# Three orders in the gated delta rule's groups: half a projection, gate 3 and the second sweep's copy moved

## What is computed

```python
qkvz = x @ W_qkvz                                     # per group: q, k, 2 x v, 2 x z
qkv = jax.nn.silu(_causal_conv1d(qkv, conv_weight))   # 4 taps
q = _l2norm(q) * Dk ** (-0.5); k = _l2norm(k)
decay_mask = jnp.exp(jnp.clip(g[..., :, None] - g[..., None, :], -30.0, 30.0))
attn = -(jnp.einsum('bhcid,bhcjd->bhcij', k_beta, k) * decay_mask)   # lower triangle
attn, _ = jax.lax.scan(_correct_row, attn, jnp.arange(1, chunk_size))  # (I + A)^-1
value_corrected = jnp.einsum('bhcij,bhcjd->bhcid', attn, v_beta)
def chunk_step(state, c): ...                         # a recurrence over the chunks
core = _rmsnorm(core * jax.nn.silu(z), norm_weight)
out = core.reshape(Bx, Sx, VAL_DIM) @ W_out
```

## Time and profile before

| | us |
|---|---|
| Timed runs, median of 3 | 1745.14 (1734.08 to 1746.89) |
| The profiled execution | 1761.52 |
| Its span, first to last instruction | 1759.8 |
| PE busy in the span | 1443.5 |
| VectorE busy | 1135.3 |
| ScalarE busy | 852.7 |
| GpSimd busy | 781.1 |

### The profile page before, as it was taken

How to read it: one execution, slowest core, us unless ns; L and a number is a source line. 1 busy time by engine, 2 the same in 40 slices (tenths; PEclk the granted TensorE clock), 3 DMA queues, 4 the chain that set the end, 5 groups by cost and what they waited for, 6 DMA issues and landing times. The chain is left out here.

```text
span 1759.8 us, 38626 instructions
## 1 busy us (share of the span) xinstructions
PE 1443.5 (82%) x14345; PEld 1032.2 (59%) x14345; DVE 1135.3 (65%) x2336; ACT 852.7 (48%) x2401; POOL 781.1 (44%) x1116
## 2 busy tenths in 40 slices
PE   5988982378624798999999999999999999986665
PEld 2543341245412466677677677777767767775465
DVE  5885138622456576787786787787778778743623
ACT  2335851132113555656655656766665665643122
POOL 6000000465201464665555555666467556453343
PEclk9999995588867898999999999999999999978688
DMA  8100005165613534645555555554464554432783
GB/s 284 54 2 2 1 4 147 31 195 166 216 53 71 129 93 124 161 117 150 142 150 117 140 151 120 151 160 113 140 173 119 152 149 127 107 92 76 202 266 126
DMA packets 249435, 218.74 MB, mean 124 GB/s; under 512 B 88770, under 2 KB 224962, under 8 KB 247200
## 3 DMA queue, kind: packets, MB, share of 16 engines
q1 hardware_dynamic: 234992, 192.41, 39.8%
q0 software_dynamic: 5712, 15.60, 2.7%
q10 hardware_dynamic: 8544, 8.26, 1.5%
HBM read 133.85 MB, written 82.25 MB: 123 GB/s over the span
## 5 line engine op out<-in xcount | busy, mean ns | idle before, releaser
L1674 PE MATMUL d_big<-all_xn_t,all_w 128*128 128x512 f32 x512 | 264.2, 649 | 27.8 <-DVE d_conv L1892 21.4
L1892 DVE SCALAR_TENSOR_TENSOR d_conv<-d_big,all_cw,d_conv 128x1023 f32<-128x1023 f32 (+2 forms) x192 | 245.4, 1278 | 48.0 <-ACT d_conv L2056 45.6
L2242 POOL TENSOR_TENSOR d_y<-d_y,all_xn 128x256 f32<-128x256 f32 x128 | 96.0, 750 | 183.6 <-DVE d_y L2033 153.2
L1674 PEld LDWEIGHTS d_big<-all_xn_t,all_w 128*128 128x128 f32 x512 | 98.3, 207 | 119.6 <-issue 97.0
L2156 ACT COPY d_ys<-d_big 128x128 f32<-128x128 f32 x256 | 61.0, 267 | 198.2 <-PE d_big L1825 139.1
L1863 PE MATMUL d_big<-all_wo,d_yt 128*128 128x256 f32 x512 | 125.7, 391 | 13.7 <-DVE d_yt L1962 13.7
L1796 PE MATMUL d_big<-all_w,all_xn_t 128*128 128x256 f32 x512 | 126.0, 390 | 0.0
L1936 DVE SCALAR_TENSOR_TENSOR d_AI<-d_big,d_b_col,d_decay 128x256 f32<-128x256 f32 x256 | 105.7, 474 | 27.0 <-PE d_big L1687 23.4
L1863 PEld LDWEIGHTS d_big<-all_wo,d_yt 128*128 128x128 f32 x512 | 96.9, 197 | 26.2 <-issue 14.2
L1796 PEld LDWEIGHTS d_big<-all_w,all_xn_t 128*128 128x128 f32 x512 | 94.5, 192 | 18.9 <-issue 7.2
L347 DVE TENSOR_REDUCE a_neg_max<-a_big 128x1 f32<-128x128 f32 (+7 forms) x128 | 90.3, 751 | 12.9 <-PE a_big L276 12.8
(11 more groups left out here) (443 smaller groups left out, 3513.7 us busy)
## 6 DMA issues: line engine op xcount, KB each, us to landing
turned_kq_scratch<-d_turned SPq DMA_DIRECT2D x32, 512.0 KB
d_kq_tok<-turned_kq_scratch SPq DMA_DIRECT2D x128, 128.0 KB
turned_v_scratch<-d_vs SPq DMA_DIRECT2D x16, 1024.0 KB
d_vs<-turned_v_scratch SPq DMA_DIRECT2D x64, 256.0 KB
grouped_y_scratch<-d_yx SPq DMA_DIRECT2D x32, 512.0 KB
d_yx<-grouped_y_scratch SPq DMA_DIRECT2D x128, 128.0 KB
all_w<-in_L_attn_W_qkvz SPq DMA_DIRECT2D x16, 768.0 KB
l_hold<-in_L_ffn_gate_up_proj SPq DMA_DIRECT2D x48, 192.0 KB
```

Of the source, the lines that this page charges most:

```text
L1674: mm = pe.matmul(big[0][:, c, :], w_sb[par][:, k, n * DK:(n + 1) * DK], xn_t[:, k, c * 512:(c + 1) * 512], start=(k == 0), stop=(k == KD - 1))
L1892: dve.scalar_tensor_tensor(conv[:, sh:T], src[:, 0:T - sh], cw[:, bass.ds(g, 1), COLUMN_OF[j], 3 - sh], conv[:, sh:T], ALU.mult, ALU.add). ...
L2242: pool.tensor_tensor(part, part, zs[:, t, :], ALU.mult).then_inc(s["yg_s"], 1)
```

## The change

Three of the lists are changed; no step is added or taken out.

- PE: half 0 of the next group's projection 2 goes ahead of `l1p`. Half 1 stays between `l1p` and `l1y`.
- ScalarE: `gates 3` goes from behind the exponentials to right behind the SiLU of projection 1. Two of the next group's square-sum steps (`ksq 0, ksq 1`) go ahead of `l1p` and two behind it, where it was three and one.
- VectorE: the copy `l2p` goes ahead of the next group's products 0.

```diff
@@ PE_ORDER
-    l0y 2, gates 2, l0y 3, l0y 4, l0y 5, l0y 6, l0y 7, gates 3; prev iv 7; this l1p 0, l1p 1, l1p 2, l1p 3; next proj 2
-    0, proj 2 1; this l1y 0, l1y 1, l1y 2, l1y 3; next products 0; this l2p 0, l2p 1; next products 1, products 2; this
+    l0y 2, gates 2, l0y 3, l0y 4, l0y 5, l0y 6, l0y 7, gates 3; prev iv 7; next proj 2 0; this l1p 0, l1p 1, l1p 2, l1p 3;
+    next proj 2 1; this l1y 0, l1y 1, l1y 2, l1y 3; next products 0; this l2p 0, l2p 1; next products 1, products 2; this
@@ DVE_ORDER
-    this l1p; prev y_turn 0; next kb; this l1y; next products 0; this l2p; next products 1; this l2y; next products 2;
+    this l1p; prev y_turn 0; next kb; this l1y, l2p; next products 0, products 1; this l2y; next products 2;
@@ ACT_ORDER
-    this gates 1; prev sq2 4, o1 7; next tap0 1; prev sq2 5; this gates 2, l0y; next silu 1, ksq 0, ksq 1, ksq 2; this
-    l1p; next ksq 3, decay; this gates 3, l1y, l2p; prev sq2 6, sq2 7; this l2y, ys 0; next tap0 2; this ys 1, o1 1;
+    this gates 1; prev sq2 4, o1 7; next tap0 1; prev sq2 5; this gates 2, l0y; next silu 1; this gates 3; next ksq 0, ksq 1; this
+    l1p; next ksq 2, ksq 3, decay; this l1y, l2p; prev sq2 6, sq2 7; this l2y, ys 0; next tap0 2; this ys 1, o1 1;
```

## The result

The changed kernel takes 1780.45 us (median of 4 runs, 1775.94 to 1788.31), the kernel before 1739.61 in the same comparison: the ratio is 1.0239, with a 95% interval of 1.0171 to 1.0307, so 30 to 53 us slower. The prediction had the sign and the mechanism, but 16 us; 1780 lies outside of its range. The profiled execution took 1784.47 us (span 1782.7).

The account below looks back on a forecast made before the run. PE was taken as the bound, busy 898.5 of 950 us. Terms -6.1 (free groups), +3.0 (five waiting), 0 (four hidden), +19.2 (six slow stretches) made +16: 1761 us, range 1727 to 1774.

Parts of the forecast that it names:

- The gap filled, l1y at 2.95: PE before l1p: half a projection (1.8) fits the 1.90 us idle, so l1y may start 2.95 behind l1p.
- Clean groups, y 0 at 13.33, bound by the chain to the exponentials: Groups without packet waits: ScalarE's chain leaves 0.53 us of the 1.8; y 0 starts at 13.33, before 13.86.
- The moved table load costs nothing: ScalarE's second table load (1.28) moves into the recurrence, where 1.7 us idle covers it: 0, upper end 7 us in all.
- Nine tied groups, whose waits replace the gain: In nine of 14 groups l1y ends only when its instruction packet arrives; earlier starts lengthen waits to 3 to 5 us.
- the five "free" ones: The five groups whose l1y is free of the packet, one clean, two slow before, two with packet in l2p: -6.1 us.
- The packets' date doesn't move (0): PE's packets queue behind the turned values, issued before l1p, and still arrive 6.6 to 8.6 us behind l1p.
- Six new slow stretches at 3.2 (+19.2): Longer waits in l1y drop PE to half clock in groups 736, 861, 993, 1185, 1248, 1438: 3.2 us each, +19.2.
- the three that had wait and slow clock already (1.8 predicted): Tied groups already waiting in l1y: VectorE's new order costs 0.6 us a group.
- packets earlier: Rival: packets come earlier as PE asks earlier, 20 us faster, 1725 us; chance 0.20.
- clock kept up: Rival: packets tied, but the clock stays up through the waits: -3, 1742 us; chance 0.32 together with fewer tied groups.
- fewer tied groups: Rival: packets' ends fall elsewhere, each tied group worth 4; six instead of nine, about 1749 us; chance 0.32 with clock kept up.
- ScalarE's gate 3 as a mere shift within its chain: Gate 3 (0.6) behind the SiLU: exponentials 1.0 us later, l1y copies 1.0 earlier.

Follow-up runs that it names:

- the two lists alone: ScalarE's and VectorE's new orders with PE's old order, against the kernel before: 1772.74 us, ratio 1.0072.
- the gap of 13 increments: Changed kernel, padded so no packet ends in the sweep, 13 of 59 semaphore increments a group moved ahead of l1y: 1794.6 us, executed once.
- The gap runs: Changed kernel padded to keep packets clear, with 13 or 24 of its 59 increments a group put ahead of l1y: 1794.6 and 1842.0 us.
- two values of one number: Changed kernel with 59 increments a group and 211 or 95 once in the first group's projections: 1765.88 or 1833.24 us, ratios 1.0012 and 1.0380.
- The run with PE's order alone and clear packets: Kernel before with only PE's new order, plus 59 increments a group and 211 in idle places: 1770.26 us, ratio 1.0041.
- The trace with padding: Changed kernel with 59 increments a group and 211 once: 1765.88 us with those in the first group's projections, 1741.01 in idle places.
- a quarter of the load: Load of the turned values cut to a quarter: changed kernel 1770.98 us, ratio 1.0058; kernel before 1747.03, ratio 0.9914.

## Why the prediction was right about the sign and wrong about the size

- **The gap filled, l1y at 2.95:** right, 3.04 in twelve groups and 3.2 in two.
- **Clean groups, y 0 at 13.33, bound by the chain to the exponentials:** right, 13.40 to 13.46 in three; the short waits at l2p and at the third product are there, 0.47 and 0.48. The table's load started at 4.08 (4.16 predicted), the exponentials ended at 7.50 (7.62).
- **The moved table load costs nothing:** right in the trace. Clean groups are 61.4 to 62.0 long (before 61.9 to 62.1), the shortest shorter by 0.46, as y 0 is earlier by 0.46. The Trainium skill (ScalarE: Activation LUTs, section "What ACT_TABLE_LOAD costs") adds a drain of about 1.38 us to the load. The exponentials start 0.01 behind their load, so the trace doesn't agree.
- **Nine tied groups, whose waits replace the gain:** right. The nine have waits of 2.8 to 4.8; a tenth (1323), counted as free, got a wait of 1.3 in l2p and 6.8 us of slow clock, +2.9 alone. So the five "free" ones brought -3.2 instead of -6.1.
- **The packets' date doesn't move (0):** not quite. Product 0 starts later in five of the nine (861, 1185, 1248, 1438, 1502: by 0.6 to 1.8) and sooner in four, together +3.6. The first packet behind l1p starts 5.1 us behind it on the mean of the nine, where it was 4.7: an earlier l1y didn't bring it sooner.
- **Six new slow stretches at 3.2 (+19.2):** this is the step that failed most, a mis-sized term. The stretches came, in the six groups named. From product 0 to y 0 these took 12.5, 11.7, 11.9, 14.8, 12.3 and 14.8, where they took 7.96: 30.2 together, where I had 20.4 (19.2, and 0.6 in each of two groups). VectorE's order is 4.5 of it, by the 0.75 a group that the runs show where the clock stays up (8.71 from product 0 to y 0, in the two lists alone and behind the gap of 13 increments). I had left it out in four of the six. The clock is the other 25.7. I priced a stretch of 6 us; they were 10.2 long, two of them 20.5. The four cost 3.0 to 3.8, near my 3.2; the two cost 6.1 each. The gap runs give like prices without a packet: 3.9 and 4.0 for 10.2 us, 5.7 for 17.1.
- **The first group:** left out of the sum without a reason. It lost 5.3 us, to GpSimd's scaling on top of the key factors.

By these terms the 14 groups have -3.2, +3.6, +30.2, and +2.2 for the three that had wait and slow clock already (1.8 predicted): 33 against 16. The 25 us between 16 and 41 are thus 9.8 in the six groups, 3.6 for the later packets, 3 in the free groups, 0.4 in the three, 5.3 in the first group and 2.0 behind the stage; these terms leave out the last 1. The terms' upper end was 32, but I ran the range only to 1774.

The rivals: packets earlier, clock kept up, and fewer tied groups all have rows against them (packets at 5.1 for 4.7, a slow clock with every packet wait of over 1.2 us in the changed kernel, nine waits). What I had not weighed is that the packets' place in the program is worth more than the edit: 80 us between two values of one number (867.9 against 948.1).

I also treated ScalarE's gate 3 as a mere shift within its chain. The run with PE's order alone and clear packets shows that it is needed: without it PE waits for its bank.

The trace with padding agrees with the Trainium skill (Advanced Engine Details and Errata, section "ISA Cache": 256 instructions a line, 16 KB): 1,155 increments more made 119 packets of 115. The prediction took from it that there are only two lines; the same section also gives 128 KB for TensorE, which doesn't fit with two lines of 16 KB, and no run here counts lines.

## What to carry to other kernels

Where an engine issues hundreds of small instructions beside heavy DMA traffic, find the packets of its instructions in the trace before judging an order: a gap closed there may only be a wait moved. If a loop's instruction count is padded to whole packets and their ends are put where nothing loads, orders can be compared fairly, and the padding may itself be the gain. In these traces the price of a slow clock differed with what followed the idle time: a gap of 1.9 us cost 0 to 3.2 us of clock in front of two half projections with 512 columns, one of 1.7 up to 5.7 in front of small tiles.

## What the runs showed of the hardware

- An "issue" wait for a packet ends 2.2 to 2.9 us behind the start of the packet's transfer. The transfer starts late behind other traffic: 4.0 to 6.3 us behind l1p in the nine tied groups, 1.1 to 1.9 in ten groups with a quarter of the load.
- A semaphore increment on PE with nothing to wait for takes 0.151 us from one to the next where PE has no matmuls queued; 7 or 8 behind 1.8 us of projection cost nothing to be seen (a clean group stayed at 61.4).
- The clock fell with idle time alone, without a wait for a packet, in 14 of 14 groups at 3.4 us and in 9 of 14 at 1.7. It then stayed at 1.2 GHz for 6.8 to 17.1 us, although PE was busy throughout (10.20 of 10.20 in the window above). One packet wait of 2.2 us left it up, so the length of the gap alone doesn't decide.
- A VectorE operation on 16 columns with two SBUF inputs took ten times as long under a GpSimd multiplication. The Trainium skill (SBUF — State Buffer, section "SBUF: two separate sides") has the two engines share a pair of ports, which a GpSimd operation or a VectorE operation with two SBUF inputs holds for a whole instruction while the other waits. The trace agrees: 0.17 and 1.72.
